# Preparing two of eight input sequences ahead of the attention loop, and the other six inside it

## What is computed

```
x = x + layernorm(attn(layernorm(x)))
x = x + layernorm(ffn(layernorm(x)))

def attn(x):                       # H = 16 heads, DH = 64, complex q, k, v
    q, k, v = x @ Wq, x @ Wk, x @ Wv
    qr, kr = q * phase, k * phase  # phase = cos + i sin of token * omega
    s = real(qr . conj(kr));  qn = |q|^2;  kn = |k|^2
    maha = max(qn + E^2 * kn - 2 * E * s, 0) / V      # E, V depend on the distance i - j
    logits = coef * log1p(maha / nu) - 0.5 * DH * log(V)
    A = softmax(causal(logits))
    return concat(real(A @ v), imag(A @ v)) @ Wo
def ffn(x): return (silu(x @ wg.T) * (x @ wu.T)) @ wd.T
```

## Time and profile before

| | us |
|---|---|
| three runs: lowest, median, highest | 1927.64, 1933.94, 1935.28 |
| the profiled execution, device time | 1928.72 |
| its span, first to last instruction | 1926.9 |
| PE busy in the span | 1800.5 (93%) |
| DVE busy | 1598.9 (83%) |
| ACT busy | 1577.4 (82%) |
| POOL busy | 1467.1 (76%) |
| first `bounds` (start of iteration 0) | 109.31 |
| iteration in the steady state, `bounds` to `bounds` | 25.1 |

### The profile page before, as it was taken

One profiled execution on the slowest core, in us unless ns is written; L12 is line 12 of the kernel. 1 busy time (PEld: TensorE's weight loads), 2 busy tenths in 40 slices (PEclk: granted clock), 3 DMA queues, 4 the chain that ended last, 5 costly groups with the idle time before them and its releaser, 6 DMA issues. The chain is left out here.

```text
span 1926.9 us, 41354 instructions
## 1 busy us (share of the span) xinstructions
PE 1800.5 (93%) x10660; PEld 1481.0 (77%) x10660; DVE 1598.9 (83%) x3838; ACT 1577.4 (82%) x3224; POOL 1467.1 (76%) x1299
## 2 busy tenths in 40 slices
PE   2379999999999999999999999999999999998997
PEld 1358888888878888887788888888888888876876
DVE  6458888888888888888788888888888898896884
ACT  5548888889888888898888888888888888886654
POOL 2278888888878888888778888888888888872654
PEclk9879999999999999999999999999999999999999
DMA  6612310131112201231112111311131101110111
GB/s 206 238 39 78 91 45 24 45 109 61 45 46 97 73 25 43 77 93 45 46 65 92 39 43 45 109 61 45 45 104 50 38 31 43 44 45 22 45 45 44
DMA packets 62093, 124.49 MB, mean 65 GB/s; under 512 B 13472, under 2 KB 42912, under 8 KB 52944
## 3 DMA queue, kind: packets, MB, share of 16 engines
q1 hardware_dynamic: 61904, 122.33, 18.9%
HBM read 106.46 MB, written 21.36 MB: 66 GB/s over the span
## 5 line engine op out<-in xcount | busy, mean ns | idle before, releaser
L586 POOL TENSOR_TENSOR qk<-rm 64x512 f32<-64x512 f32 x512 | 692.6, 1353 | 102.6 <-PE ps L790 42.4
L596 POOL TENSOR_TENSOR ek<-tabs,kn 128x512 f32<-128x512 f32 (+3 forms) x512 | 463.3, 912 | 133.5 <-DVE lg L1468 93.1
L750 PE MATMUL pa<-xt,wt 128*128 128x512 f32 x1536 | 437.8, 421 | 10.7 <-issue 6.6
L1476 DVE CUSTOM_DVE_ANT_0 lg<-lg,tabs,ncog 128x512 f32<-128x512 f32 (+3 forms) x512 | 438.3, 874 | 0.0
L1443 DVE TENSOR_TENSOR rm<-pa,tabs 128x512 f32<-128x512 f32 x512 | 332.0, 676 | 76.6 <-POOL qk L586 68.6
L1468 DVE CUSTOM_DVE_ANT_0 lg<-ps,ek,qb 128x512 f32<-128x512 f32 (+3 forms) x512 | 279.2, 545 | 128.8 <-POOL ek L596 86.7
L790 PE MATMUL ps<-qk 128*128 128x512 f32 (+3 forms) x1024 | 375.6, 451 | 8.9 <-DVE lg L1468 7.4
L814 PE MATMUL py<-pt,vt 128*128 128x128 f32 x2560 | 347.8, 275 | 0.1
L814 PEld LDWEIGHTS py<-pt,vt 128*128 128x128 f32 x2560 | 330.7, 191 | 16.3 <-issue 0.3
L750 PEld LDWEIGHTS pa<-xt,wt 128*128 128x128 f32 x1536 | 284.5, 192 | 66.2 <-issue 13.2
L1117 ACT ACTIVATE lg<-lg,qb 128x512 f32<-128x512 f32 (+3 forms) x512 | 278.8, 558 | 15.2 <-DVE lg L1468 11.5
(11 more groups left out here) (162 smaller groups left out, 2160.2 us busy)
## 6 DMA issues: line engine op xcount, KB each, us to landing
xt<-xs_d SPq DMA_DIRECT2D x62, 1024.0 KB, 4.8
tabs<-vec_d SPq DMA_DIRECT2D x8, 1536.0 KB, 8.6
xs_d<-xt SPq DMA_DIRECT2D x8, 1024.0 KB, 4.8
wt<-wraw_d SPq DMA_DIRECT2D x7, 768.0 KB, 5.9
acc<-in_L_attn_x SPq DMA_DIRECT2D x8, 512.0 KB, 5.8
tabs<-rope_d SPq DMA_DIRECT2D x64, 64.0 KB, 4.3
tabs<-in_L_attn_x SPq DMA_DIRECT2D x8, 512.0 KB, 4.6
out<-tabs SPq DMA_DIRECT2D x8, 512.0 KB, 3.2
```

Source lines behind the costliest of these rows:

```text
L586: pool.tensor_tensor(qk[part * DH:(part + 1) * DH, z * HH + hh, :], rm[row, 2 * part, :], rm[row, 2 * part + 1, :], ALU.add if part else A ...
L596: pool.tensor_tensor(ek[:, n % 2, 0:w], tab(par, hh, E2_T, w), kn[:, hh, 0:w], ALU.mult).then_inc(ek_pool, 1)
L750: last = mm(pa[r][:, :], wproj(par, z, kt, a, r * P, (r + 1) * P), xt[slot][:, kt, b, :], start=(n == 0), stop=(n == 3 * KT - 1))
L1476: dve.tensor_tensor_reduce(lg[:, hh, at(n)], lg[:, hh, at(n)], tab(par, hh, T3_T, w), ncog[:, par, 0, hh:hh + 1], 3e38, ALU.add, ALU.min, ...
```

## The change

Only sequences 0 and 1 are normalised, transposed and split ahead of the loop. The other six are handled in iterations 0 to 5: iteration `t` transposes and splits sequence `t` + 2, and projections of the first group read the split buffers straight (`xbuf`, three of them, the third being `hx`), not what SP loads back.

In detail:

- Normalising no longer uses ACT and the scratch: DVE (sequences 0 and 1) or POOL (2 to 7) subtracts and multiplies in place in `acc` (`x_normal`). The first `add_output` of a sequence in group 0 writes instead of adding (`over`), so `acc` isn't cleared.
- Inside an iteration `x_turn` (4 transposes, twice) goes through the one bank `po`, which `out_project` also uses; `x_high` and `x_low` are put into ACT's and DVE's order, twice each. Iterations 0 and 2 also get `x_stats` on DVE and `x_rstd` on POOL; iterations 0 to 4 get `x_normal` on POOL, between `decay_norm(c, 1, 3)` and `decay_norm(cn, 0, 0)`.
- The first 9 iterations are written out with constant counts; the hardware loops start behind them.
- The order ahead of the loop is new. The small parameter loads are issued by ACT. SP loads the FFN weights early. The rotation tables of group 0 are computed straight into `tabs[0]` (an extra `rope_angle(-1)` and `group_trig`); the four parts for the other groups follow during the priming, with 5 instead of 7 DVE instructions and 4 instead of 5 on ACT each, in two alternating buffers. The nine `ffn_turn`s stand between the projections.

```
+XBUF = 3
...
+        ffn_raw = [tabs[1][:, 0:3, :], tabs[1][:, 3:6, :],
...
+                          own=own, x=t % XBUF if t < B else t % 2, xn=(t + 1) % XBUF if t + 1 < B else (t + 1) % 2, over=True)
+
+            for t in range(B + 1):
...
             with eng.Fori(0, G // 2 - 1) as gg:
+                group(gg, 1, False)
                 group(gg, 0, False)
-                group(gg, 1, False)
-            group(G // 2 - 1, 0, False)
             group(G // 2 - 1, 1, True)
...
+            x_load(0)
+            x_load(1)
+            stage_weights()
+            for raw, w, parts in ((ffn_raw[0], wg_d, FT), (ffn_raw[1], wu_d, FT), (ffn_raw[2], wd_d, KT)):
+                sp.dma_start(raw.rearrange("p a n -> p (a n)").bitcast(I32).rearrange("p (r n) -> p r n", r=parts),
+                             w.rearrange("(r p) n -> p r n", p=P)).then_inc(ffn_in, 16)
+            x_load(2)
+            x_load(3)
...
+            sp.wait_ge(vec_out, 64)
+            load_decay(0, 0)
+            sp.dma_start(nco[:, :, :], bass.AP(tensor=nco_d.tensor, offset=0, ap=[[0, P], [3, H], [1, 3]])).then_inc(nco_in, 16)
+            for b in range(4, B):
+                x_load(b)
+            load_output_weights(0)
             x_store(0)
...
+            for k in range(ROPES):
+                rope_store(k)
...
+                if t < B - 2:
+                    x_store(t + 2)
                 sp.wait_ge(v_rdy, (t + 1) * 2 + 2)
...
+                if t >= B - 2:
+                    load_x((t + 2) % B, t % 2)
...
+            def x_normal(n):
+                for j in range(NT):
+                    q = n * NT + j
+                    last = pool.tensor_scalar(acc[:, n, j, :], acc[:, n, j, :], mv[:, q, 0:1], rstd[:, q:q + 1], ALU.subtract, ALU.mult)
+                last.then_inc(x_norm, 1)
...
+                if it.own in (1, 3):
+                    x_rstd(it.own // 2 + 2)
+                    x_settled(it.own // 2 + 2)
+                if it.own is not None and it.own < B - 2:
+                    x_normal(it.own + 2)
...
+            x_settled(1)
+            x_normal(2)
...
+            def x_turn(c, n, kt):
                 pe.wait_ge(x_norm, n + 1)
-                for kt in range(KT):
-                    if n >= 2:
-                        pe.wait_ge(x_hi, 2 * (n - 2) + kt + 3)
-                        pe.wait_ge(x_lo, 2 * (n - 2) + kt + 3)
-                    for j in range(NT):
-                        last = pe.transpose((pa, pp)[n % 2][kt][:, j * P:(j + 1) * P], xnorm[n % 2][:, j, kt * P:(kt + 1) * P],
-                                            ident[:, :])
-                    last.then_inc(x_tr, 1)
...
+                if n < 2:
+                    dst = (pa, pp)[n][kt]
+                else:
+                    dst = po
+                    if kt == 0:
+                        if c[4]:
+                            pe.wait_ge(acc_dve, c[4])
+                    else:
+                        pe.wait_ge(x_lo, 2 * n + 1)
+                for j in range(NT):
+                    last = pe.transpose(dst[:, j * P:(j + 1) * P], acc[:, n, j, kt * P:(kt + 1) * P], ident[:, :])
+                last.then_inc(x_tr, 1)
...
+                    if own is not None:
+                        pe.wait_ge(x_lo, 2 * own + 2)
+                    else:
+                        pe.wait_ge(xt_in[slot], v if isinstance(v, int) else pe.snap(v))
...
+                if it.own is not None and it.own < B - 1:
+                    x_turn(cp, it.own + 1, 0)
...
+                if it.own is not None and it.own < B - 1:
+                    x_turn(cp, it.own + 1, 1)
...
+                if it.own is not None and it.own < B - 1:
+                    pe.wait_ge(x_lo, 2 * it.own + 4)
...
+            c0 = counts(pe, 0, PERS)
+            x_turn(c0, 0, 0)
+            x_turn(c0, 0, 1)
+            x_turn(c0, 1, 0)
+            x_turn(c0, 1, 1)
+            pe.wait_ge(w_lo, KT)
+            project(c0, 0, 0, 0, 0, 0, 0, 0)
+            project(c0, 0, 0, 0, 0, 0, 0, 1)
             pe.wait_ge(w_lo, 3 * KT)
-            c0 = counts(pe, 0, PERS)
-            project(c0, 0, 0, 0, 0, 0)
-            project(c0, 0, 0, 0, 0, 1)
-            project(c0, 0, 0, 0, 1, 0)
-            project(c0, 0, 0, 0, 1, 1)
+            ffn_turn(0)
+            ffn_turn(1)
+            ffn_turn(2)
+            project(c0, 0, 0, 0, 0, 0, 1, 0)
+            project(c0, 0, 0, 0, 0, 0, 1, 1)
+            for n in range(3, 9):
+                ffn_turn(n)
             norms_k(c0)
+            pe.wait_ge(ffn_ev, 9)
             scores(c0, 0, 0)
             norm_q(c0)
             scores(c0, 0, 1)
             scores(c0, 0, 2)
+            pe.wait_ge(w_in[0], 16 * WEIGHT_LOADS)
             run_iterations(pe, body)
...
+            act.wait_ge(p_load, 16 * 6)
             a_step(act.activation(hp[:, 6:11], hp[:, 0:5], ACT.Abs))
             a_step(act.activation(hp[:, 11:16], hp[:, 6:11], ACT.Exp, scale=-1.0))
-            a_step(act.activation(hp[:, 16:21], hp[:, 11:16], ACT.Ln, bias=1.0))
             act.wait_ge(p_dve, V_EXP)
             a_step(act.activation(v_e, v_e, ACT.Exp))
+            a_step(act.activation(hp[:, 16:21], hp[:, 11:16], ACT.Ln, bias=1.0))
...
+            def group_trig():
+                act.wait_ge(rope_dve, 5)
+                act.activation(ropet(0, 1), ang[0], ACT.Sin).then_inc(rope_act, 1)
+                act.activation(abs_ang, ang[0], ACT.Abs).then_inc(rope_act, 1)
+                act.wait_ge(rope_act, 2)
+                act.activation(ropet(0, 0), abs_ang, ACT.Sin, bias=half_pi[:, :], scale=-1.0).then_inc(rope_act, 1)
+
+            def rope_trig(k):
+                act.wait_ge(rope_dve, 5 * (k + 2))
+                if k == 0:
+                    act.wait_ge(vec_out, 64)
+                if k >= 2:
+                    act.wait_ge(rope_out[k - 2], 48)
+                act.activation(rope_sp[k % 2], ang[(k + 1) % 2], ACT.Sin).then_inc(rope_act, 1)
+                act.activation(rope_sn[k % 2], ang[(k + 1) % 2], ACT.Sin, scale=-1.0).then_inc(rope_act, 1)
+                act.wait_ge(rope_act, 4 * k + 3)
...
+                act.wait_ge(rope_act, 4 * k + 6)
+                act.activation(rope_cs[k % 2], abs_ang, ACT.Sin, bias=half_pi[:, :], scale=-1.0).then_inc(rope_act, 1)
...
+            x_high(0, 0)
+            x_high(0, 1)
+            group_trig()
+            x_high(1, 0)
+            x_high(1, 1)
...
+                if it.own is not None and it.own < B - 1:
+                    x_high(it.own + 1, 0)
...
+                if it.own is not None and it.own < B - 1:
+                    x_high(it.own + 1, 1)
...
+                if it.before is None:
+                    for k in range(ROPES):
+                        act.wait_ge(rope_out[k], 48)
...
             square(c0, 0, 0)
             square(c0, 0, 1)
+            for n in range(3):
+                ffn_keep(n)
+            rope_trig(0)
             square(c0, 1, 0)
             square(c0, 1, 1)
+            for n in range(3, 9):
+                ffn_keep(n)
+            rope_trig(1)
+            rope_trig(2)
+            rope_trig(3)
+            act.wait_ge(ncog_dve, 1)
...
+            def x_normal(n):
+                if n == 0:
+                    dve.wait_ge(x_root, 1)
+                for j in range(NT):
+                    q = n * NT + j
+                    last = ts(acc[:, n, j, :], acc[:, n, j, :], mv[:, q, 0:1], rstd[:, q:q + 1], ALU.subtract, ALU.mult)
+                last.then_inc(x_norm, 1)
...
+            x_normal(0)
...
             def rope_angle(k):
-                z = ang[k % 2]
-                if k >= 2:
-                    dve.wait_ge(rope_act, 5 * (k - 1))
-                rope_step(ts(z, tokens, om[:, k:k + 1], None, ALU.mult))
-                rope_step(ts(turns, z, 1.0 / (2 * math.pi), MAGIC, ALU.mult, ALU.add))
-                rope_step(ts(turns, turns, MAGIC, None, ALU.subtract))
-                for c in TWO_PI:
-                    rope_step(stt(z, turns, -c, z, ALU.mult, ALU.add))
+                z = ang[(k + 1) % 2]
+                if k >= 1:
+                    dve.wait_ge(rope_act, 3 if k == 1 else 4 * (k - 1) + 3)
+                q = k % (ROPES + 1)
+                rope_step(ts(turns, tokens, om2[:, q:q + 1], MAGIC, ALU.mult, ALU.add))
+                rope_step(ts(turns, turns, MAGIC, -TURN, ALU.subtract, ALU.mult))
+                rope_step(stt(z, tokens, om[:, q:q + 1], turns, ALU.mult, ALU.add))
+                rope_step(stt(z, turns, REST / TURN, z, ALU.mult, ALU.add))
...
-            x_move(0)
-            rope_angle(0)
-            x_stats(1)
...
+            def x_low(n, kt):
+                dve.wait_ge(x_hi, 2 * n + kt + 1)
+                tt(xbuf[n % XBUF][:, kt, 1, :], ((pa, pp)[n][kt] if n < 2 else po)[:, :], xbuf[n % XBUF][:, kt, 0, :].bitcast(F32),
+                   ALU.subtract).then_inc(x_lo, 1)
+
+            rope_angle(-1)
+            x_low(0, 0)
+            x_low(0, 1)
+            x_normal(1)
```

(18 more changed lines are left out.)

346 lines of the change are left out of this document (130 added, 216 removed).

## The result

The changed kernel is slower, by two thirds of a percent: 1944.8 us median (1942.7 to 1945.93) beside 1932.3 for the kernel before, a ratio of 1.0065 with a 95% interval of 1.0047 to 1.0084. The prediction, 1909 with a range of 1896 to 1922, was wrong in size and in sign. The profiled execution has a span of 1941.0 us, 14.1 over that of before.

The account below looks back on a forecast made before the run. PE was taken to bound the loop and a chain of waits from engine to engine the start-up. Start-up gain 42.8 less 18.3 given back is 24.5: 1904.2 for the profiled execution, 1909 for the median, range 1896 to 1922.

Parts of the forecast that it names:

- Small tables at 24.5: Start-up: the small tables are ready at 24.5 us, as in the kernel before.
- the lower bound of 34: Start-up: least gain, if one `rope_store` takes 9.3 us and parameter loads land 2 us later; 42.8 was forecast.
- rival (2): Start-up is longer: its ping-pong has no slack, three steps wait on DMAs; gain 34, time 1918; chance 0.14.
- rival (4): Iterations 0 to 5: PE loses its clock, 18.6 us more per iteration wholly at 1.2 GHz, all six 2021; chance 0.03.
- The terms behind `rope_trig(3)`: End of the start-up: `keep_norm_k` 0.6 and `norm_q` 1.7 after 63.7, putting the first `bounds` at 66.5.
- (c): Loop: `x_normal` on POOL takes 1.5 us, at most 2.9, and is covered by 1.2 plus 0.3, so costs nothing.
- (a): Loop: eight transposes on PE in each of six iterations, 0.88 us each iteration.
- (b): Loop: two `x_high` on ACT and two `x_low` on DVE put 0.8 us onto PE's path in each of six iterations.
- Rival (3): Loop: PE stands still for both copies through bank `po`, 15.1 us in place of 4.8; time 1919; chance 0.09.
- (d): Iterations 0 and 2: `x_stats` on DVE lets 2.5 us through and `x_rstd` on POOL 1.6, together 4.1, twice.
- (e): Rest of the loop: written-out iterations and SP's changed stores and loads of `x` cost nothing.
- the 0.92 for faster: Chance given to a time of 1924 or below, counted as faster than the kernel before.

Follow-up runs that it names:

- s1: The kernel after, with POOL's six subtractions of `low_weights` started only when DVE has finished the small tables; tables at 25.0, first `bounds` at 74.57.
- k1: The kernel after, with POOL's own start-up work (six subtractions, three casts, `x_normal(2)`) left out; first `bounds` at 68.06, time 1936.8 us.
- e4: The kernel after, with sequences 3 to 7 normalised on ACT in four spread places, not on POOL; 1915.0 us, ratio to before 0.9931.
- d1: The kernel before, with two added POOL instructions of 128x256 ahead of `decay_norm(cn, 0, 0)` in every iteration, forms alternating; 1992.2 us beside 1927.8.
- p1: The kernel after, with `x_normal` of sequences 3 to 7 still on POOL but spread over four places; 1922.7 us, ratio to before 0.9968.
- e1: The kernel after, with sequences 3 to 7 normalised on DVE at the place of `x_stats`, not on POOL; 1928.3 us, ratio to before 1.0004.

## Why the prediction was wrong, point by point

**What bounds the kernel, and that the start-up is a chain that gets shorter:** right. It gave 34.5 us.

**Small tables at 24.5: wrong, 30.6.** The step read the price of each DVE instruction from a time in which POOL was idle, and did not ask what POOL does at the new place. From there on the order of the steps was as put and each was later: last sines at 72.1, not 63.7. s1 and k1 show that 6.7 of the 8.3 us are POOL's. The waits on DMAs, from which the lower bound of 34 was made, were not the cause: ahead of its last sines ACT waits 0.68 for DVE's angle, not for a store; rival (2) was right in size (34) and wrong in its reason.

**Readings that don't hold, though little hangs on them.** The "0.97 at the low clock" for four transposes: the granted clock of the kernel before is 1.00 from 27 to 29 us. "4.82 cold" for twelve projections: the clock is 0.50 there up to 90.6 and rises behind that; in the kernel after the first twelve took 3.75, at 1.00. The price in rival (4), 1.74, sets that beside 1.38 from another view; like with like it is 3.12 to 1.64, 1.9 times. The terms behind `rope_trig(3)`, 63.7 + 0.6 + 1.7, make 66.0 and not 66.5. And the 0.1 that is added for each of the four instructions in (c) stands in no row.

**(a) and (b), turns and splitting: right**, 10.1 predicted, 11.0 measured on e4, 12.1 beside the wait on POOL. Rival (3), a PE that stands still for both copies, would have been 5.3 + 15.1; it fell.

**(c) `x_normal` on POOL: the step that failed**, 0 predicted, 26.6 measured. Three errors are in it. First the duration: it was taken from rows of other forms, an in-order cast and a subtraction, and called bounded by them; the form has 1.22, 1.7 times the upper one. The nearest row is no bound if its form isn't the same. With 4.9 for the four and its own cover of 1.5, the prediction would have had 3.4 in each of five iterations, 17. Then the cover: 1.2 + 0.3 was read, and in d1 2.2 of 2.46 us went through. And the place: it is the one in POOL's order with a waiting DVE and a waiting PE behind it, and p1 shows that three quarters of the cost go when the block is taken apart and moved.

The sentence of the prediction that DVE and POOL block each other on SBUF ("SBUF — State Buffer" of the Trainium skill, "Who interferes with whom") is about a DVE operation with two SBUF inputs, and was weighed for `logits` in the loop, 0.8 each time. No such lengthening shows: `x_normal` has a median of 1.22 in the kernel after and 1.22 to 1.23 in d1. It was DVE that was held up, in the start-up and in e1: most of all its `tensor_scalar`s, which have one tensor input (1.37 and 4.42 for four), and some steps of the angles with two (1.64 for 0.75). The rule of the same skill's "GPSIMD Engine Reference", section 4.1, of roughly line rate for one input isn't borne out for this form: 4.8 ns per column against 1.6 for a copy (1.22 and 0.40 us over 256 columns).

**(d) Statistics: right**, 8.2 predicted, 7.3 measured, as far as single executions tell.

**(e) Everything else at nothing: wrong by 6.6.** 3.5 of it are the two closings of the outer loop, with the clock at 0.89 in both (62.3 against 58.8); 2.3 is the rest of the loop, mostly one weight-splitting iteration per group of 26.5 instead of 26.2, and 0.7 lies behind the last `bounds`. What causes the 0.3 in the splits was not tried.

**Rival (4), the clock, had a part.** Stretches 3, 4 and 5 are at 0.90, 0.90 and 0.95; without the wait on POOL (e4) the stretches of iterations 2 to 5 are at 1.00, as in the earlier trace rows. Stretch 2, which is as long as these, is at 1.00. The clock is an addition to some of the long waits of PE, not a state into which the kernel falls.

**The sum.** 8.3 in the start-up, 23.7 in the six stretches (42.0 against 18.3) and 6.6 behind them are 38.6: the distance from the predicted span, 1904.2 less 1.8, to 1941.0. **The chances** were wrong as well: the 0.92 for faster rested on bounds of unknown prices that were too narrow, and no rival had POOL as the engine on which the others wait. The condition under which the forecast would be wrong (over 30 in the iterations) was met by (c) and the rest together.

## What to carry to other kernels

Before work is moved into a full loop, look at what stands behind the new place in that engine's own order and who waits for it: the same 4.9 us on POOL, done in five iterations, cost 26.6 us in one block ahead of the instruction on which DVE and PE waited, and 6.2 in four places. Of an instruction form that the trace does not have on that engine, measure the price first; a copy, a cast and a two-input operation bounded nothing. And before work goes to DVE or POOL, look at what the other does at that moment: a block of four `tensor_scalar`s on DVE took 1.37 us or 4.42, by whether POOL was at work. The same work cost 11.5 us as a block on DVE and next to nothing in four places on ACT.

## What the runs showed of the hardware

On POOL, `tensor_scalar` of 128x256 with two per-row operands takes 1.22 to 1.23 us, with one constant 0.86, a copy 0.40 (d1), so the form with one tensor input is slower than a two-input `tensor_tensor` (0.73 in the kernel before). Four DVE `tensor_scalar`s of 128x256 take 1.37 us while POOL is idle and 4.42 while POOL works, 0.34 and 1.1 each (e1), and POOL's `x_normal` beside DVE's angles took 6.01 instead of 4.9 (after). Behind a wait of PE of 3.0 us, in which the granted clock was 1.00, it was 0.50 for the next 3 us (after, 241.6 to 248.1). At the four closings of a hardware loop PE paused for 3.13, 3.16, 3.23 and 3.45 us, and the clock of the stretch was 0.89, 1.00, 0.89 and 0.94 (after, before, after, before): pauses of nearly one length were followed by either.
